# One block of edge weights by sixteen small instructions instead of one large one

## What is computed

```python
W = jnp.einsum('rb,bio->rio', comp, basis)          # 8 types out of 4 bases
h_all = jnp.einsum('ni,rio->nro', node_feats, W)
msgs = h_all[src, edge_types]
agg = jax.ops.segment_sum(msgs, dst, num_segments=node_feats.shape[0])
```

## Time and profile before

| | |
|---|---|
| median of 3 runs | 628.27 us (625.47 to 629.73) |
| the profiled execution | 628.48 us, of which the span from first to last instruction is 626.7 us |
| PE busy | 535.3 us, 85% of the span |
| POOL busy | 432.5 us, 69% |
| DVE busy | 380.1 us, 61% |

### The profile page before, as it was taken

How to read it: one execution, slowest core, us unless ns; L and a number is a source line. 1 busy time by engine, 2 the same in 40 slices (tenths; PEclk the granted TensorE clock), 3 DMA queues, 4 the chain that set the end, 5 groups by cost and what they waited for, 6 DMA issues and landing times.

```text
span 626.7 us, 10679 instructions
## 1 busy us (share of the span) xinstructions
PE 535.3 (85%) x3189; PEld 436.9 (70%) x3189; DVE 380.1 (61%) x1410; ACT 204.4 (33%) x411; POOL 432.5 (69%) x448
## 2 busy tenths in 40 slices
PE   0667898999999876998999999999999983389990
PEld 0566797888877765777787878788787851268880
DVE  6869887544433344554666566766666666626882
ACT  6672622210033010132424242424334331155430
POOL 7777777777777777777777777777777710474662
PEclk9969999999999988999999999999999976599996
DMA  8994333333333354334444444445454518474221
GB/s 279 271 264 123 102 102 102 100 102 99 94 105 106 102 163 140 101 115 139 138 149 146 140 143 144 150 136 151 130 157 127 153 62 246 126 208 117 80 85 41
DMA packets 41362, 85.24 MB, mean 136 GB/s; under 512 B 10793, under 2 KB 23018, under 8 KB 41107
## 3 DMA queue, kind: packets, MB, share of 16 engines
q0 software_dynamic: 21920, 60.90, 33.4%
q1 hardware_dynamic: 18372, 22.95, 11.6%
q10 hardware_dynamic: 1008, 0.65, 0.3%
HBM read 71.66 MB, written 12.81 MB: 135 GB/s over the span
## 4 chain that ended last, share of the span: by engine, by line
PE 64%; DVE 11%; DMA 9%; POOL 7%; issue 5%; ACT 1%; DVEq 0%; ACTq 0%; POOLq 0%
PE ps L930 26%; PE ps L992 12%; DMA gath<-xn_d,src_i 7%; PE ps L981 6%; POOL gath L592 5%; PE ps L1208 3%; PE ps L1199 3%; PE ps L958 3%; POOL both L638 2%; PE ps L947 2%; PE ps L968 2%; DVE raw_stats L1316 2%; PE ps L1015 1%; DMA rel_of<-in_relation_of 1%; PE ps L891 1%
## 5 line engine op out<-in xcount | busy, mean ns | idle before, releaser
L592 POOL DMA_INDIRECT gath<-xn_d,src_i x263 | 253.2, 963 | 80.1 <-issue 67.6
L930 PE MATMUL ps<-wmat,gath 128*128 128x80 f32 (+1 forms) x1052 | 155.0, 288 | 14.8 <-DMA gath<-xn_d,src_i 13.9
L930 PEld LDWEIGHTS ps<-wmat,gath 128*128 128x128 f32 x1052 | 139.4, 194 | 33.0 <-DMA gath<-xn_d,src_i 19.7
L1386 DVE TENSOR_TENSOR wmat<-hit,wts 128x576 f32<-128x576 f32 (+1 forms) x100 | 63.1, 631 | 130.3 <-PE ps L930 130.1
L592 POOL DMA_INDIRECT acc_raw<-xn_d,src_i x96 | 96.4, 1004 | 29.3 <-issue 21.0
L1411 DVE TENSOR_TENSOR acc_raw<-acc_raw,ps 128x144 f32 (+1 forms) x392 | 88.3, 266 | 40.7 <-PE ps L930 39.8
L930 PE MATMUL ps<-wmat,acc_raw 128*128 128x144 f32 x512 | 76.7, 294 | 8.2 <-ACT acc_raw L700 7.7
L930 PEld LDWEIGHTS ps<-wmat,acc_raw 128*128 128x128 f32 x512 | 69.6, 192 | 14.7 <-issue 9.2
L992 PE MATMUL ps<-wk_et,acc_raw 128*128 128x256 f32 (+1 forms) x200 | 53.9, 394 | 0.0
L638 POOL DMA_INDIRECT both<-rows_d,inv_i x25 | 24.0, 959 | 43.3 <-DVE inv_i L1686 35.7
L992 PE MATMUL ps<-wq_wv,acc_raw 128*128 128x256 f32 (+1 forms) x200 | 52.2, 384 | 0.0
(11 more groups left out here) (232 smaller groups left out, 728.6 us busy)
## 6 DMA issues: line engine op xcount, KB each, us to landing
rows_d<-both SPq DMA_DIRECT2D x24, 256.0 KB, 2.5
gath<-xn_d,src_i POOLq DMA_INDIRECT x263, 2.8
both<-in_x SPq DMA_DIRECT2D x24, 128.0 KB, 3.7
both<-in_x SPq DMA_DIRECT2D x4, 640.0 KB, 9.7
xn_d<-both SPq DMA_DIRECT2D x4, 640.0 KB
acc_raw<-in_w_t SPq DMA_DIRECT2D x1, 2080.0 KB
acc_raw<-in_w_t SPq DMA_DIRECT2D x1, 2048.0 KB, 7.2
acc_raw<-xn_d,src_i POOLq DMA_INDIRECT x96, 2.8
```

What stands on the lines that cost most here:

```text
L592: g.indirect_dma_start(place_of(n), None, table, bass.IndirectOffsetOnAxis(ap=src_i[:, n:n + 1], axis=0)).then_inc(done, 16)
L930: ins = t_.matmul(ps_edge[quarter][:, m * w:(m + 1) * w], place_of(n)[:, m * P:(m + 1) * P], wmat_tiles[:, k, 0:w], start=k == pair[0], st ...
L1386: d.tensor_tensor(made, hit[:, :, 0:width(q)].unsqueeze(2).to_broadcast([P, w, B, width(q)]), wts[:, :, cut].rearrange("p b t -> p t b").u ...
```

## The change

From octet 26 on `build_hit` does nothing. `build_weights` makes, for each of the 4 tiles of its half and each of the 4 bases, one block of 128 by 20 with a single `tensor_scalar`: `iota` is compared with the partition's `rel` and the outcome multiplied with the partition's coefficient. Both scalars are columns in SBUF. The sixteenth of these gives `wmat_built`. The wait for `multiplied` stays ahead of them, the wait for `hit_built` falls away. Below octet 26 nothing changes, and the output is the same.

```diff
@@ build_hit(q, half)
+                if q >= NARROW:
+                    return
                 w = OCT // 2
@@ build_weights(q, half)
                 if not isinstance(q, int) or q > 0:
                     v.wait_ge(multiplied, OCT * q + half * w + w)
+                if q >= NARROW:
+                    for k in range(half * w, half * w + w):
+                        for b in range(B):
+                            ins = d.tensor_scalar(wmat_tiles[:, k, b * SLIM:(b + 1) * SLIM], iota[:, 0:SLIM], rel[:, OCT * q + k:OCT * q + k + 1],
+                                                  wts[:, b, OCT * q + k:OCT * q + k + 1], ALU.is_equal, ALU.mult)
+                    ins.then_inc(wmat_built, 1)
+                    return
                 v.wait_ge(hit_built, n + 1)
```

## The result

The changed kernel takes 687.39 us in the median (685.70 to 690.19), the kernel before 628.58 in the same runs: 1.0931 times as long, 95% interval 1.0900 to 1.0961. The forecast was 692 us, slower.

The account below looks back on a forecast made before the run. PE was taken to set the pace in octets 26 to 49, with DVE becoming the bound after the change: 153.6 - 27 - 76 + 13 = 63.6 us on 628.5 gives 692 us, range 655 to 735 us.

Parts of the forecast that it names:

- The step on which it hung: Price of one small two-scalar 128x20 instruction on DVE: 0.20 us start to start, bounds 0.08 and 0.28; 768 add 153.6 us.
- The overlap of 0.087 us: On DVE, the second of two L1609 instructions started 0.087 us before the first one's end; subtracted from duration to get pitch.
- DVE's slack: DVE's waits for PE before L1386 and L1411 let it take about 76 us of extra work before PE feels it.
- Break-even: Price per small instruction at which added work equals waits plus removed work: (76 + 27) / 768 = 0.134 us.
- the gathers' 13 us: GpSimd gathers hold up DVE's small instructions: about four met per octet, 0.56 us, 13 us in 24 octets; bounds 0 and 23.
- The prediction's octet of about 13 us: DVE's work per octet with the slim builds, over PE's 10.1 us, making DVE the bound from the 25th to 48th.
- What is late next: Next octet's weights, PSUM-freeing accumulations and row statistics, in DVE's order; PE waits at L930 and before L992; POOL gains slack.
- Rival 2: Dense small scalar forms keep POOL from writing; octets take 16.5 us, 154 us more, 782 us; chance 0.04.
- Rival 3: PE, busy 78%, loses its full clock; at half speed throughout 240 us more, 868 us; chance 0.02.
- the prediction allowed 15: At granted clock 0.83, PE's octet of 12.2 us stays covered by DVE; waits no longer lining up add perhaps 15 us.

## Why the prediction was right

**The step on which it hung held.** The price was put at 0.20 us per instruction from rows of other sizes: 0.55 ns a column, some 60 ns per scalar, and what is left. Measured: 0.200 us, with 60 ns per scalar and 0.5 ns per column, each taken apart by a run of its own. The overlap of 0.087 us that the prediction took from one pair holds too: median duration less pitch is 91, 89 and 89 ns with two, one and no scalars. So the forecast 768 x 0.20 = 153.6 us of work were added. That each part came out within a few ns, read from rows of other kinds and sizes, was partly luck.

**DVE's slack was the right limit.** The waits of 76 us in the stage are a stock that is used up first: half of the instructions cost 2.8 us and all of them 58.8. Break-even was put at 0.134 us; 0.139 us gave a kernel 1.6% slower and 0.080 us one 0.4% slower. Past it DVE's work shows about one to one, as the hits made again and octet 49 left out show. The stock is a little smaller than the forecast had it: by a break-even of 0.134 us the run with one scalar should have lost 768 x (0.139 - 0.134) = 3.8 us, and it lost 9.4. So some 76 - 5.6 = 70 us of the waits could be used, and the break-even lies nearer (70 + 27) / 768 = 0.126 us.

**Two terms of the sum were mis-sized and partly cancel.** The stock of waits was taken as used up to the last; 6.2 us in four waits are left, worth 6.5 us of pitch, so 69.5 were taken up, not 76, as the run with one scalar says too. The longest of the four, 2.6 us, stands ahead of the first slim build, where no small instruction had run yet to fill it. And the gathers' 13 us is the step that failed: the prediction let each lengthened instruction hold back the next. The lengthening is there, 15 us in all, but hardly moves the next start: some 2.5 us come back in the stage without gathers. With the measured terms the sum is 153.6 - 27 - 69.5 + 2.5 = 59.6 us, against 58.7 between the profiled executions. The forecast's 63.6 was 4.9 us too much, out of 10.5 too much and 6.5 too little, and the rest lies within rounding and the parts outside the stage. That these two errors have opposite signs is luck, though the two together could not have carried the forecast out of its range.

The prediction's octet of about 13 us has a slip in it: 10.1 less its three waits is 7.0, not 7.2 us. With 7.0 and without the 0.56 us for the gathers it would have been 12.3; measured are 12.4. The sum of the time does not use it.

**What is late next was named in part.** PE does wait at L992 for the accumulations (5.7 us), but most of it is at L1015, the logits, for `route` of an earlier node tile (23.8 us): `route` stands last in DVE's order. At L930, where the prediction had it wait for weights, PE's waits show none for DVE: a whole octet lies between a build and its use. POOL gains slack as said, and between 305 and 545 us it stands 60.8 us for PE:

```profile
L592 POOL DMA_INDIRECT gath<-xn_d,src_i x155 | 147.4, 951 | 93.7 <-PE ps L930 60.8 <-issue 32.9
```

**The rivals.** Rival 2, starved gathers, falls by the same line: 951 ns each, as before. Rival 3 happened in small. PE's share of busy time is 221.09 / 240.00 = 92% and not 78%. At the full clock of the earlier trace rows its 1144 matmuls would make 1144 x 191.44 / 1134 = 193 us, 80%; the rest is the granted clock, 0.91 over the stage, at which they take longer. Four windows of the changed kernel, with the columns as above, and DVE's builds in the second and right behind the fourth (of that one the view shows only the first 4 of 16):

```profile
328.00:332.00 4.00, 2.30 (x15) 1.73 (x15) 3.39 (x18) 1.45 (x3) 2.65 (x3) 1.00 0.34 98
332.80:336.20 3.40, 3.40 (x14) 3.04 (x14) 3.40 (x19) 1.28 (x1) 1.49 (x2) 0.50 0.38 125
408.00:411.00 3.00, 3.00 (x12) 2.73 (x12) 3.00 (x16) 1.16 (x1) 1.23 (x2) 0.50 0.39 131
357.00:363.00 6.00, 6.00 (x24) 5.36 (x23) 5.56 (x27) 2.04 (x4) 1.90 (x2) 0.50 0.38 120
```

```profile
332.75 3.31 DVE L1389 TENSOR_SCALAR wmat<-iota,rel,wts 128x20 f32<-128x20 f32 x16
...
363.86 0.90 DVE L1389 TENSOR_SCALAR wmat<-iota,rel,wts 128x20 f32<-128x20 f32 x4 [1.27 <-PE ps L930]
```

From 328 to 332 us PE was busy 2.30 of 4.00 us at the full clock; from 332.8 us on the clock stood at 0.50. A clock of 0.50, 1.2 of 2.4 GHz, for some 3.4 us costs nothing here: DVE is busy through the second and third windows, and PE's slower matmuls are still in time. Where it lasts through 357 to 363 us, PE's matmuls come late and DVE waits 1.27 us ahead of its second build. Three of the four waits that are left are of this size, 3.6 us in all, where the prediction allowed 15; in the 5 to 7 us ahead of the other two the clock is 0.52 and 0.50. That it is the clock which makes them late is read from the trace; no run was made with the clock held up.

## What to carry to other kernels

An engine that waits has a stock of time. Work added to it costs little until the stock is gone (2.4 us for 34 us of net work with no scalars, 2.8 us for 63 us with half of the builds), and all of it after that. Price the added instructions by the distance of their starts, not by their durations, and compare the sum with the engine's waits in that stage. Many small instructions with scalars read per partition are dear: at 20 columns two scalars were 120 of 200 ns and the columns 10. Put the same work into fewer, longer instructions first; one over 80 columns cost 213 ns.

## What the runs showed of the hardware

- A vector scalar form of 20 columns starts every 80 ns with two constants, 139 ns with one scalar read per partition and 200 ns with two; 16 more columns add 8 ns.
- An instruction whose duration a gather lengthens does not hold back the next one by as much, in a row of such instructions: 15 us more duration over 768 of them (312 instead of 292 ns), 2.5 us more time from the first to the last, and 1.8 us more in the 720 distances of starts within the builds. The single L1457 of the earlier trace rows had suggested otherwise: there the next instruction, of another kind, did start later. Why the row absorbs it was not tried.
- GpSimd's closing `DRAIN` took 9.48 us in every profile with 441 indirect DMAs, and 5.88 us in the one with 258.
